# A Mamba, attention and feed-forward tower on one core: every engine's program in a new order, with three step products side by side, PSUM banks chosen per use, and work moved off VectorE and GpSimd

## The reference, cut to what matters

```python
x = emb[ids]                                              # 16 x 128 x 192
for i in range(2):                                        # Mamba, D_INNER 384, D_STATE 16, DT_RANK 12
    xr, res = split(rmsnorm(x, norm_w[i]) @ in_proj_w[i])
    xr = silu(causal_conv4(xr) + conv_b)
    dt, B, C = split(xr @ x_proj_w)                       # 12, 16, 16
    delta = softplus(dt @ dt_proj_w + dt_proj_b)
    h[t] = exp(delta * A) * h[t-1] + delta * B * xr       # 16 states a channel
    x = x + ((C . h) + xr * D) * silu(res) @ out_proj_w
q, k, v = layernorm(x) @ w_qkv                            # 12 heads of 16
a = relu(1 + s + s*s/2), s = q.k/4;  x = x + (a / sum(a)) @ v @ w_proj + b_proj
y = layernorm(x);  x = x + bitlinear(silu(gate) * up)     # up, gate = bitlinear(y); ternary weights, 8-bit rounding a row
```

## Time and profile before

| | |
|---|---|
| median of three runs | 409.15 us |
| the profiled execution's own time | 410.43 us |
| its span, first to last instruction | 408.6 us |
| PE, DVE, ACT, POOL busy | 367.5, 322.0, 256.9, 269.1 us |
| mean granted TensorE clock | 0.962 |
| traffic with HBM | 5.87 MB read, 1.57 MB written |

### The profile page before, as it was taken

How to read it: one execution, slowest core, us unless ns; L and a number is a source line. 1 busy time by engine, 2 the same in 40 slices (tenths; PEclk the granted TensorE clock), 3 DMA queues, 4 the chain that set the end, 5 groups by cost and what they waited for, 6 DMA issues and landing times.

```text
span 408.6 us, 6845 instructions
## 1 busy us (share of the span) xinstructions
PE 367.5 (90%) x2012; PEld 207.4 (51%) x2012; DVE 322.0 (79%) x672; ACT 256.9 (63%) x495; POOL 269.1 (66%) x350
## 2 busy tenths in 40 slices
PE   0489797999999999999997899999999999999765
PEld 0324242346355453473542796684564674566554
DVE  2059999989897988998898988458687888779732
ACT  2267988787885888867967622343657575565541
POOL 5537557878797679895887875505546456748851
PEclk9999999799978999979999789999999999999999
DMA  6843000000000000000000000000000000000001
GB/s 152 216 135 62 12 0 0 1 3 0 0 2 1 1 2 0 0 3 0 2 0 2 2 0 2 0 2 2 1 2 12 11 19 4 21 10 16 26 16 36
DMA packets 7056, 7.92 MB, mean 19 GB/s; under 512 B 1614, under 2 KB 6055, under 8 KB 7016
## 3 DMA queue, kind: packets, MB, share of 16 engines
q1 hardware_dynamic: 5382, 5.71, 4.8%
q0 software_dynamic: 768, 1.57, 1.8%
q10 hardware_dynamic: 866, 0.17, 0.2%
HBM read 5.87 MB, written 1.57 MB: 18 GB/s over the span
## 4 chain that ended last, share of the span: by engine, by line
PE 71%; DVE 11%; POOL 6%; issue 6%; ACT 3%; DMA 1%; DVEq 0%; ACTq 0%; POOLq 0%
PE bank L686 10%; PE bank L836 8%; PE bank L660 6%; PE bank L690 5%; PE bank L735 5%; PE bank L750 4%; PE bank L896 4%; PE bank L927 3%; PE bank L940 3%; PE bank L977 2%; PE bank L962 2%; PE bank L899 2%; PE bank L984 2%; PE bank L676 2%; PE bank L758 2%
## 5 line engine op out<-in xcount | busy, mean ns | idle before, releaser
L1728 DVE SCALAR_TENSOR_TENSOR pair<-bank,cw,pair 128x508 f32<-128x508 f32 (+2 forms) x72 | 51.0, 731 | 11.7 <-ACT pair L308 10.7
L686 PE MATMUL bank<-ring,win 128*128 128x512 f32 x96 | 54.6, 658 | 5.5 <-DVE pair L1728 2.8
L1377 POOL TENSOR_TENSOR arena<-arena,dl 128x512 f32<-128x512 f32 x24 | 44.8, 1868 | 15.5 <-DVE dl L1720 14.3
L1383 POOL TENSOR_TENSOR du<-dl,pair 128x512 f32<-128x512 f32 x24 | 30.6, 1275 | 27.7 <-DVE dmin L1737 27.7
L660 PE MATMUL bank<-ident 128*128 128x128 f32 x266 | 40.5, 300 | 8.6 <-ACT arena L535 4.7
L660 PEld LDWEIGHTS bank<-ident 128*128 128x128 f32 x266 | 34.6, 204 | 24.0 <-issue 11.4
L1404 POOL TENSOR_TENSOR arena<-arena 128x512 f32<-128x512 f32 x24 | 36.3, 1513 | 9.9 <-DVE arena L1764 9.4
L836 PE MATMUL bank<-wout,pair 128*128 128x192 f32 x192 | 39.1, 366 | 0.0
L836 PEld LDWEIGHTS bank<-wout,pair 128*128 128x128 f32 x192 | 36.5, 218 | 1.8 <-issue 1.8
L686 PEld LDWEIGHTS bank<-ring,win 128*128 128x128 f32 x96 | 15.8, 200 | 32.7 <-issue 20.4
L490 ACT ACTIVATE du<-bank 128x512 f32<-128x512 f32 x48 | 25.1, 598 | 10.5 <-PE bank L927 10.4
(11 more groups left out here) (172 smaller groups left out, 890.2 us busy)
## 6 DMA issues: line engine op xcount, KB each, us to landing
out<-h SPq DMA_DIRECT2D x16, 96.0 KB, 1.6
win<-in_w SPq DMA_DIRECT2D x2, 384.0 KB
arena<-ffn_in_t SPq DMA_DIRECT2D x1, 768.0 KB
wout<-out_w SPq DMA_DIRECT2D x2, 288.0 KB
win_rest<-in_w SPq DMA_DIRECT2D x2, 192.0 KB
arena<-ffn_out_t SPq DMA_DIRECT2D x1, 384.0 KB
wa<-w_qkv SPq DMA_DIRECT2D x1, 384.0 KB
h<-emb,idx POOLq DMA_INDIRECT x16, 6.1
```

The source lines that it names most:

```text
L686: nc.tensor.matmul(bank[:, IN_BANKS[m], :], win[:, j // NG, m * P:(m + 1) * P], xtr[:, j % 2, m % 2, :], start=True, stop=False)
L1377: nc.gpsimd.tensor_tensor(relu_s[:, c, :], relu_s[:, c, :], dl[:, j % NG, c, :], ALU.subtract).then_inc(rest_done, 1)
L1383: nc.gpsimd.tensor_tensor(du[:, g, c, :], dl[:, g, c, :], xc[:, g, c, :], ALU.mult).then_inc(du_ready, 1)
L1728: nc.vector.scalar_tensor_tensor(acc, seqs(bank[:, X_BANKS[c], :])[:, :, 0:LEN - tap], cw[:, j // NG, c, TAPS - 1 - tap:TAPS - tap], acc, ...
```

## The change

It touches every engine.

- **Step products.** The 12 rows of dt now come out of `project_x` three times, at partitions 48, 80 and 112 (125 output rows in place of 80), and a row of ones behind each; `project_steps` issues three products with contraction over 29 rows each (the first 16 against zero weights), in row bands 32, 64 and 96, without another instruction between them. The step weights are loaded by six small DMAs on SP's queue in place of two, behind a wait for a clearing memset on DVE.
- **Logarithm in PSUM.** `one_plus` writes 1 + e^-|s| back over the step product in its PSUM bank; `error` and `delta` read it there, and `logarithm` reads and writes there.
- **Moved to ACT.** `scale` (DVE, one instruction of 768 columns a chunk; now ACT, four of 192), `take_k` (DVE) and `take_sums` (DVE, three instructions a sequence; now one ACT copy of 384 columns).
- **Value sums by TensorE.** `turn_sums` now begins with a product of ones with the values (384 columns), and the three transposes that follow accumulate on it as plain matmuls; the column of ones beside the squared scores is gone.
- **The flag.** `weakest_below` (POOL, three instructions a chunk) and `scale_squares` (POOL) are replaced by `largest_shortfall` and `raise_squares` (DVE, one instruction each a chunk); `count_short` has one matmul in place of three. The threshold goes from -104 to -110.
- **Banks per use.** Every call has its own bank from a table (`IN_BANKS[j]`, `S_BANKS[j]`, `TH_BANKS[s]` and so on).
- **Orders.** The loops over i are gone: all four compute engines follow lists written out for the whole kernel. `keep_clock` is defined and never called.

The core of the diff:

```diff
-B_AT, C_AT, DT_AT, ONE_AT, XM = 0, 32, 64, 76, 80
+B_AT, C_AT, XM = 0, 32, 125
+STEP_AT = (32, 64, 96)
+DT_IN, STEP_ROWS = 16, 29
-UNDERFLOW = -104.0
+UNDERFLOW = -110.0
-S_BANKS = (2, 4, 3)
+S_BANKS = ((0, 3, 7), (5, 0, 6), (4, 1, 7), (2, 5, 1), (5, 0, 3), (3, 6, 5), (3, 2, 5), (6, 7, 3))
...
-                nc.scalar.activation(du[:, j % NG, c, :], dl[:, j % NG, c, :], ACT.Identity,
+                nc.scalar.activation(bank[:, S_BANKS[j][c], :], dl[:, j % NG, c, :], ACT.Identity,
                                      bias=1.0).then_inc(u1_done, 1)
...
-                nc.scalar.activation(du[:, j % NG, c, :], du[:, j % NG, c, :], ACT.Ln).then_inc(ln_done, 1)
+                nc.scalar.activation(bank[:, S_BANKS[j][c], :], bank[:, S_BANKS[j][c], :], ACT.Ln).then_inc(ln_done, 1)
...
+            def scale(j):
+                act.wait_ge(rstd_ready, j + 1)
+                for i in range(SG):
+                    t = j % NG * SG + i
+                    last = nc.scalar.activation(xsr[:, j % 2, i, :], h[:, t, :], ACT.Identity, scale=rstd[:, t:t + 1])
+                last.then_inc(xs_ready, 1)
...
+            def take_sums(s):
...
+                nc.scalar.activation(nm[:, s % 2, :, :], bank[:, PV_BANKS[s], 0:CH * P].rearrange("p (c n) -> p c n", n=P),
+                                     ACT.Copy).then_inc(nm_out, 1)
...
-            def project_steps(j, c):
...
-                nc.tensor.matmul(bank[:, S_BANKS[c], :], wdt[DT_AT:DT_AT + R + 1, j // NG, c * P:(c + 1) * P],
-                                 dbl[DT_AT:DT_AT + R + 1, j % 2, :], start=True, stop=True).then_inc(s_ready, 1)
+            def project_steps(j):
+                pe.wait_ge(dbl_ready, j + 1)
+                for c, at in enumerate(STEP_AT):
+                    nc.tensor.matmul(bank[:, S_BANKS[j][c], :], wdt[at:at + STEP_ROWS, j // NG, c * P:(c + 1) * P],
+                                     dbl[at:at + STEP_ROWS, j % 2, :], start=True, stop=True).then_inc(s_ready, 1)
...
             def turn_sums(s):
-                pe.wait_ge(nm_out, CH * s + CH)
+                b, i = seat(s)
+                pe.wait_ge(nm_out, s + 1)
+                nc.tensor.matmul(bank[:, SUM_BANKS[s], 0:CH * P], ones[:, :], va[b][:, i, :, :].rearrange("p h w -> p (h w)"),
+                                 start=True, stop=False)
                 for c in range(CH):
-                    last = nc.tensor.transpose(bank[:, A_BANK, c * P:(c + 1) * P], nm[:, s % 2, c, :], ident[:, :])
+                    last = nc.tensor.matmul(bank[:, SUM_BANKS[s], c * P:(c + 1) * P], nm[:, s % 2, c, :], ident[:, :],
+                                            start=False, stop=(c == CH - 1))
                 last.then_inc(nm_turned, 1)
...
-                nc.vector.scalar_tensor_tensor(dl[:, g, c, :], du[:, g, c, :], 1.0, dl[:, g, c, :],
+                nc.vector.scalar_tensor_tensor(dl[:, g, c, :], bank[:, S_BANKS[j][c], :], 1.0, dl[:, g, c, :],
                                                ALU.subtract, ALU.subtract).then_inc(err_done, 1)
```

More of the change, by code:

```diff
@@ new lines, in _ @@
+            raise_squares(3)
+            convolve(1, 2, 3)
+            ternary_weights()
+            b_times_c(0)
+            convolve(2, 0, 1)
+            error(0, 0)
+            convolve(2, 0, 2)
+            convolve(2, 1, 1)
+            convolve(2, 0, 3)
+            convolve(2, 1, 2)
+            delta(0, 0)
+            convolve(2, 1, 3)
+            error(0, 1)
+            b_times_c(1)
+            error(0, 2)
+            convolve(2, 2, 1)
+            delta(0, 1)
+            convolve(2, 2, 2)
@@ new lines, in _ @@
+            error(2, 1)
+            delta(1, 2)
+            largest_shortfall(1)
+            scan_first(1, 1)
+            delta(2, 0)
+            add_h(0, 0)
+            add_h(0, 1)
+            times_c(1, 1)
+            memoryless_states(1, 2)
+            input_times_b(1, 2)
+            raise_squares(4)
+            scan_first(1, 2)
+            skip(1, 2)
+            error(2, 2)
+            convolve(3, 0, 1)
+            delta(2, 1)
+            times_c(1, 2)
+            raise_flag(1)
@@ new lines, in _ @@
+            convolve(4, 2, 1)
+            convolve(4, 0, 3)
+            convolve(4, 2, 2)
+            convolve(4, 2, 3)
+            delta(3, 0)
+            add_h(1, 0)
+            error(3, 1)
+            add_h(1, 1)
+            error(3, 2)
+            input_times_b(3, 0)
+            delta(3, 1)
+            raise_squares(5)
+            b_times_c(4)
+            memoryless_states(3, 0)
+            scan_first(3, 0)
+            delta(3, 2)
+            times_c(3, 0)
+            add_h(2, 0)
@@ new lines, in _ @@
+            input_times_b(3, 1)
+            skip(3, 0)
+            memoryless_states(3, 1)
+            scan_first(3, 1)
+            error(4, 0)
+            memoryless_states(3, 2)
+            add_h(2, 1)
+            input_times_b(3, 2)
+            delta(4, 0)
+            skip(3, 1)
+            scan_first(3, 2)
+            raise_squares(6)
+            error(4, 1)
+            times_c(3, 1)
+            times_c(3, 2)
+            error(4, 2)
+            skip(3, 2)
+            largest_shortfall(3)
@@ new lines, in _ @@
+            convolve(6, 1, 2)
+            add_h(3, 0)
+            convolve(6, 1, 3)
+            convolve(6, 0, 2)
+            convolve(6, 2, 1)
+            error(5, 0)
+            convolve(6, 0, 3)
+            add_h(3, 1)
+            error(5, 1)
+            convolve(6, 2, 2)
+            delta(5, 0)
+            convolve(6, 2, 3)
+            delta(5, 1)
+            error(5, 2)
+            input_times_b(5, 0)
+            raise_squares(7)
+            memoryless_states(5, 0)
+            input_times_b(5, 1)
@@ new lines, in _ @@
+            error(6, 0)
+            times_c(5, 1)
+            times_c(5, 2)
+            states_dve(5)
+            delta(6, 0)
+            error(6, 1)
+            convolve(7, 0, 1)
+            convolve(7, 1, 1)
+            error(6, 2)
+            convolve(7, 1, 2)
+            convolve(7, 0, 2)
+            convolve(7, 1, 3)
+            convolve(7, 0, 3)
+            normalise(1)
+            normalise(2)
+            normalise(3)
+            convolve(7, 2, 1)
+            delta(6, 1)
@@ L2026, in _ @@
+            scan_first(6, 2)
+            add_h(5, 1)
+            error(7, 0)
+            raise_flag(6)
+            times_c(6, 1)
+            times_c(6, 2)
+            skip(6, 2)
+            error(7, 1)
             error(7, 2)
+            states_dve(6)
+            take_v(0, 0)
+            take_v(0, 1)
             delta(7, 0)
[L2028 to L2031 removed]
+            delta(7, 1)
+            delta(7, 2)
+            variances(1)
```

2769 lines of the change are left out of this document (1662 added, 1107 removed).

## The result

The changed kernel takes **394.12 us** (median of 4, 393.07 to 396.22); the kernel before took 409.19 beside it. The ratio is 0.9649, with a 95% interval of 0.9604 to 0.9694: 15 us faster, where 379 was forecast. The profiled execution took 396.22 us, 394.2 of them span; TensorE's mean granted clock over it is 0.908 (0.962 before).

The account below looks back on a forecast made before the run. DVE, with ACT close behind, bounds the first stretch, which ends at 24 + 1 + 217 = 242 us; then PE is full for 130 and the tail takes 7. Forecast 379 us, range (8 in 10) 356 to 401.

Parts of the forecast that it names:

- the sum for the rest: From chunk 7's end on: PE has 125 us of work, 96% full, so 130, plus 7 at the end, 137 us.
- the rival of the falling clock: With the fillers gone the clock falls and PE's work behind the seam (248 us) runs slower: 422 us, chance 0.07.
- The sign that I named: The forecast is wrong if the clock is low for more than some 20 us in all.
- PE's fillers, 28.3 us: Unused PE products in the chunks and just ahead of 248 us: removing them takes 28.3 us off PE's busy time.
- The step products: Each chunk's three products run side by side on PE, 1.07 us instead of 2.99, saving 15.4 us in all.
- nothing is lost but room: If step products don't overlap, PE has 15.4 us more in the first stretch, yet the kernel takes 379 to 384.
- DVE: First stretch, the Mamba chunks: 198 us of DVE work at 91% full, so the stretch takes 217 us.
- 6 us sooner than now: The first stretch ends at 242 us, against 248 now, though it takes in 26 us of PE's later work.
- The start: The first stretch, beginning at 24 us, starts 0 to 3 us later; 1 us was taken.
- The value sums: Products of ones on PE, 0.7 us a sequence, and 0.4 more for three matmuls replacing transposes: 16 x 1.1 = 17.6 us.
- the signs: What the trace was to show if the forecast held, among it value sums at 1.4 us a sequence.
- The tail: After PE's last dense work, the chain of the last sequences takes 7 us, between 2 and 10.6.

Follow-up runs that it names:

- scores_ahead: The changed kernel with scores waiting for the squares of the sequence before the last, not of the last: 375.44 us, 0.9192 of the kernel before.
- early_ahead: The changed kernel with that shorter wait for squares in sequences 0 to 3 alone: 394.42 us, 0.9637 of the kernel before.
- fill_scores: The changed kernel with its waits kept and six unused products of 0.25 us in each gap ahead of scores: 388.82 us, 0.9494 of the kernel before.
- before_no_fill: The kernel before with none of its fillers, nothing else changed: 412.83 us, 1.0069 of the kernel before.
- rows_first: The changed kernel with two PE calls swapped, so chunk 0 finishes its first two banks before the next two begin: 394.28 us, 0.9640 of the kernel before.
- ahead_taps_first: scores_ahead with the two PE calls of rows_first swapped and two first taps on ACT moved ahead of scale(1): 376.81 us, 0.9198 of the kernel before.

## Why the prediction was wrong

The direction and the range held; the size did not, a gain of 15 us where 30 were forecast.

**The step that failed** is the one in the sum for the rest: "PE: 125 us, full, at the 96% it has now: 130." The work was there, and even less of it: 127.5 us of busy time, 119.7 where the clock stays up (`scores_ahead`). The 96% was not: PE was 92% busy from the flag to 374 us and 54% behind that, since the 96% belonged to the old order, in which other work follows every scores call. The rest took 146.3 us in place of 137. I took the share of one order and put it on another without reading what each function waits for at its first line. The same wait, at the scores of group 0, also made chunk 7 late, 247.9 us in place of 242 (`early_ahead`, which frees only these, has 242.7). With the wait taken back to what the banks need, the kernel takes 375.4 us, with chunk 7 done at 242.4 (242 forecast) and 130 us behind it (137 forecast). So the forecast was near the kernel without the leftover wait, but some of that is luck: ahead of the flag 5 us more of DVE's work and a later start met an engine 95% full where 91% was taken, and behind it PE was 99% full with 5 us less to do.

**What the wait costs** is 19 us, not the 10.5 of its six gaps: about 11.6 are idle time, 7.6 are work at the lower level of the clock. That is the rival of the falling clock, in small: the mean granted clock is 0.908, against 0.962 before, and with levels of 0.50 and 1.00 only that is 73 us at the low one (0.092 x 394 x 2) against 31. I gave it 0.07 as one case for the whole kernel; it came as an addition to another case. The sign that I named, more than some 20 us at the low clock, did show, but it was badly set: the kernel before had 31 already. `fill_scores` prices what the gaps let fall at 5.5 us. The Trainium skill's page "TensorE: Matmul & The Clock Gate", section "Part 1", says that the low level is the default and that activity releases it; useless products in the gaps raise the clock from 0.95 or 0.97 to 1.00 behind the flag, so here the runs agree.

**PE's fillers, 28.3 us.** The busy time fell as forecast, but `before_no_fill` shows that this was no price: taken alone it saves nothing and costs 0.7%. 9.7 us of the fillers covered a wait for DVE, and without them the clock was 0.88 in place of 0.93. That the sum came out right for the changed kernel is likely because its order has attention's work in these gaps; no run took the fillers and the order apart.

**The step products.** They run side by side, 1.06 to 1.21 us a chunk at full clock (1.07 forecast). On what that is worth I was wrong: I had "nothing is lost but room", 0 to 5 us, if they did not; it is 13.3 us. A stage that lies on each chunk's chain is not free just because its engine is only 85% full. The Trainium skill's page "TensorEngine Tiling (Array Packing)", section "Key Properties", says that a change of tiling mode drains TensorE. The rows above have such a change from row bands to all 128 rows at 132.18 us: the next product starts 1.06 us after the step products did, within their own 1.13, so no cost of it is seen here.

**DVE.** 203.8 us of work against 198, at 93% against 91%: the stretch from 28 to 247.9 us is 220 us long, 217 forecast. The 6 us too few come from the marker: the sum takes 248 us as the end of the chunks, and the flag of chunk 7 stood at 258.62. Up to there DVE had 214.3 us, not 207.1, and the same sum gives 206. For the same reason the forecast of a first stretch "6 us sooner than now" compares two different points. `error` and `delta` were 0.05 us better than taken; the scan was 0.15 worse, 24 times, 3.6 us. The slow scans stand beside a POOL instruction; that the overlap is the cause was not tried.

**The start** was 3.1 us later, 27.79 against 24.74 us for the first convolution, where I took 1. Another order of PE's first projections and of ACT's taps gets back 1 to 2 us of it (26.60 us in `rows_first`, 26.24 in `ahead_taps_first`), and three runs find that this changes nothing at the end; the rest of the delay was not followed.

**The value sums** took 0.65 us for the product of ones (0.7 forecast) and 0.66 for the three with the identity, 1.31 in all where the signs had 1.4 (the 0.4 in the sum is only what the three cost more than the transposes before), from start to start in PE's timeline of `scores_ahead`:

```profile
276.26 0.81 PE L1135 MATMUL bank<-du,ones 128*128 128x384 f32 x2
276.91 0.83 PE L1138 MATMUL bank<-ident,arena 128*128 128x128 f32 x6
277.57 1.03 PE L1167 MATMUL bank<-wq,arena 96*128 96x512 bf16 x4
```

I had 11.2 us for the sixteen products of ones; leaving them out takes 7.0 us off PE's busy time and 4.8 off the kernel. PE's busy time bounds that stretch less strictly than its 99% says: once it has less to do, it waits.

**The tail** was to be 7 us beside dense work. Here, in the last 20.2 us, PE idles for 9.2, and raising the clock there changes 1.1 to 1.2 us: POOL, with 13.5 of 20.2 us, and the chain over it are likelier to set the rest, which was not tried.

`scores_ahead` beats both kernels: 0.9192 of the kernel before, 19 us under the changed one.

## What to carry to other kernels

When an order is laid out anew, list the first wait of each function and ask which of them the new banks still need: a wait that the old order covered costs nothing until its neighbour moves, and the share an engine reaches in one order need not hold in the next. Price a gap on TensorE at its length plus the work that runs at the lower clock behind it, here roughly half as much again (5.5 us of clock to 13.4 of the rest in one reckoning, 7.6 to 11.6 in the other). And before counting removed fillers as a gain, ask which wait each of them stood in.

## What the runs showed that I had not expected

A lead can be lost to the clock: `early_ahead` reached the seam 5.9 us sooner and ended at the same time, with 6.0 us more of busy time for the same instructions. And with DVE at 95% and PE at 85%, 15 to 16 us more on either cost 13 us: in this kernel, where three engines work through a chunk in fixed orders, no single bound could be read from the shares.
